# Attention values in quarters of the array, behind the query projections

## What is computed

```
x = x + _L0_conv_ref(_gn(x), ...)      # window attention and ffn
x = x + _L1_conv_ref(_gn(x), ...)      # patch network
# in the first, for windows of 8 x 8 pixels and 4 heads of 16 channels:
qkv = xw @ qkv_w + qkv_b
q, k, v = jnp.split(qkv, 3, axis=-1)
scores = jnp.einsum('bhqd,bhkd->bhqk', q, k)     # divided by the norms of q and k, and by tau
attn = jax.nn.softmax(scores + bias + mask)
out = jnp.einsum('bhqk,bhkd->bhqd', attn, v)
out = out.transpose(0, 2, 1, 3).reshape(B * NW, TOK, C) @ proj_w + proj_b
```

## Time and profile before

| | us |
|---|---|
| median of 3 runs | 784.1 |
| lowest, highest | 783.03, 784.84 |
| span of the profiled execution | 778.6 |
| TensorE busy | 665.7 (86%) |
| VectorE busy | 516.4 (66%) |
| ScalarE busy | 480.4 (62%) |
| GpSimd busy | 355.1 (46%) |

### The profile page before, as it was taken

The page is one execution under the profiler, slowest core; times in us unless marked ns, Lnnn a source line. Parts: engine busy times, 40 slices in busy tenths (PEclk is TensorE's granted clock), DMA queues, the critical chain, the costliest instruction groups (busy, mean ns, idle before and its releaser), DMA issues. The chain is left out here.

```text
span 778.6 us, 21192 instructions
## 1 busy us (share of the span) xinstructions
PE 665.7 (86%) x8584; PEld 371.4 (48%) x8584; DVE 516.4 (66%) x997; ACT 480.4 (62%) x963; POOL 355.1 (46%) x441
## 2 busy tenths in 40 slices
PE   4785789999999999999998579999999988749880
PEld 2562455565565555655555232233333367735350
DVE  4796487877777787877778322577777786372181
ACT  3565266777777777777775548877777656624000
POOL 4696446778777777788776520022221123100000
PEclk9787599999999999999999959999999999969955
DMA  9550000000000000000000020122112220120278
GB/s 216 137 128 11 1 3 2 3 2 3 2 3 3 3 3 3 3 2 3 3 2 3 2 56 1 28 55 56 33 50 55 55 55 2 31 72 2 63 194 269
DMA packets 15719, 31.44 MB, mean 40 GB/s; under 512 B 7488, under 2 KB 9284, under 8 KB 15620
## 3 DMA queue, kind: packets, MB, share of 16 engines
q1 hardware_dynamic: 12592, 29.16, 14.1%
q10 hardware_dynamic: 2760, 0.66, 0.5%
q0 software_dynamic: 272, 0.27, 0.2%
HBM read 20.71 MB, written 9.37 MB: 39 GB/s over the span
## 5 line engine op out<-in xcount | busy, mean ns | idle before, releaser
L794 POOL TENSOR_TENSOR sc<-sc,mx 128x512 f32<-128x512 f32 x128 | 133.7, 1044 | 102.4 <-DVE mx L725 102.4
L722 DVE TENSOR_TENSOR sc<-s_ps,bias_tab 128x512 f32<-128x512 f32 x128 | 87.7, 685 | 52.6 <-PE s_ps L528 52.6
L1424 POOL TENSOR_TENSOR square<-xs 128x1024 f32<-128x1024 f32 x16 | 34.1, 2133 | 165.5 <-DVE xs L1166 165.5
L539 PE MATMUL t_ps<-consts,sc 128*128 128x128 f32 x512 | 84.4, 288 | 16.2 <-ACT pt L656 12.5
L656 ACT ACTIVATE pt<-t_ps 128x512 f32<-128x512 f32 x128 | 75.7, 592 | 31.2 <-PE t_ps L539 30.1
L539 PEld LDWEIGHTS t_ps<-consts,sc 128*128 128x128 f32 x512 | 54.3, 142 | 84.8 <-issue 48.1
L725 DVE TENSOR_REDUCE mx<-sc 128x8 f32<-128x512 f32 x128 | 87.8, 686 | 4.4
L1081 ACT ACTIVATE hs<-h_ps,fb1s 128x512 f32<-128x512 f32 x128 | 78.2, 689 | 19.1 <-PE h_ps L990 19.0
L528 PE MATMUL s_ps<-kx,qu 32*64 32x128 f32 x2048 | 72.3, 278 | 3.5 <-DVE kx L749 2.9
L990 PE MATMUL h_ps<-xs,fw 64*128 64x512 f32 x256 | 68.7, 650 | 1.0 <-ACT hs L1081 1.0
L528 PEld LDWEIGHTS s_ps<-kx,qu 32*64 32x64 f32 x2048 | 56.7, 134 | 15.2 <-issue 13.4
(11 more groups left out here) (207 smaller groups left out, 1295.2 us busy)
## 6 DMA issues: line engine op xcount, KB each, us to landing
raw<-in_x_dram SPq DMA_DIRECT2D x32, 256.0 KB, 5.1
xr<-in_x_dram SPq DMA_DIRECT2D x32, 256.0 KB, 3.9
out_dram<-x SPq DMA_DIRECT2D x32, 256.0 KB, 3.9
rec_scratch<-r SPq DMA_DIRECT2D x4, 224.0 KB, 2.5
w<-in_L_conv_W_dram SPq DMA_DIRECT2D x1, 784.0 KB
w<-in_L_conv_W_dram SPq DMA_DIRECT2D x1, 672.0 KB
xs<-rec_scratch SPq DMA_DIRECT2D x16, 28.0 KB
xs<-rec_scratch ACTq DMA_DIRECT2D x16, 28.0 KB
```

The source lines that it names most:

```text
L539: last = pe.transpose(t_ps[:, m], sc[n % KEPT][:, m].rearrange("c h k -> c (h k)"), ident)
L722: dve.tensor_tensor(sc[n % KEPT][:, :, :, :], s_ps[j][:, :, :, :], bias_tab[:, j, hp], ALU.add)\
L794: pool.tensor_tensor(v, v, mx[n % KEPT][:, :].unsqueeze(2).broadcast_to([128, 8, TOK]), ALU.subtract)\
```

## The change

The value weights wv are no longer a 128 x 128 tile with zero blocks but 128 x 64, the weights once on each half of the rows; the memset of wv and its semaphore go. `values` takes one window of one image at a time (64 rows, 64 tokens) against 64 columns of weights. Where there were eight products over the whole array, there are 32, in turn on the four quarters. Bank a_ps[0] now holds the values of the lower image and a_ps[1] those of the upper, for both j; before, bank j held both images. `spread_values` copies by image accordingly, in the same number of operations of the same size. In `tensor_step` `values` moves from behind `turn(n - 2, 1)` to ahead of it, directly behind `project_queries`. In `scalar_step` the second `copy_queries` moves from the start of the next step to behind the first one, ahead of an exponent.

```
-        wv = sb(attention, "wv", [128, 128])
+        wv = sb(attention, "wv", [128, C])
...
-                          (wv[lo:hi, lo:hi], qkv_w[:, 2 * C:3 * C]), (pw[lo:hi, :], proj_w)]
+                          (wv[lo:hi, :], qkv_w[:, 2 * C:3 * C]), (pw[lo:hi, :], proj_w)]
...
-                    pool.memset(wv[:, :], 0.0).then_inc(zeroed, 1)
-                    pool.wait_ge(zeroed, 1)
...
                     for j in range(2):
                         for n in range(4):
-                            cols = slice(128 * n, 128 * (n + 1))
-                            last = pe.matmul(a_ps[j][:, cols], xu[:, 2 * p + j, cols], wv[:, :], start=True, stop=True)
+                            for w, (to_lo, to_hi) in enumerate(HALVES):
+                                at = slice(TOK * (2 * n + w), TOK * (2 * n + w + 1))
+                                for a, (lo, hi) in enumerate(HALVES):
+                                    last = pe.matmul(a_ps[a][to_lo:to_hi, C * (4 * j + n):C * (4 * j + n + 1)],
+                                                     xu[lo:hi, 2 * p + j, at], wv[lo:hi, :], start=True, stop=True)
...
-            def spread_values(act, p, j):
+            def spread_values(act, p, a):
...
-                    v = a_ps[j][:, :].rearrange("c (n g h d) -> c n g h d", n=4, g=4, h=2)
-                    to = vd[p % 2][:, WIN * j:WIN * (j + 1)].rearrange("c (n w) a p d -> c n w (a p) d", w=2)
+                    v = a_ps[a][:, :].rearrange("c (n g h d) -> c n g h d", n=8, g=2, h=2)
+                    to = vd[p % 2][:, :, a].rearrange("c (n w) p d -> c n w p d", w=2)
...
                 project_queries(pe, n - 1)
+                values(pe, n - 1)
                 turn(pe, n - 2, 1)
-                values(pe, n - 1)
                 score(pe, n - 2, 2)
...
-                copy_queries(act, n - 2, 1)
                 spread_values(act, n - 2, 0)
...
                 copy_queries(act, n - 1, 0)
+                copy_queries(act, n - 1, 1)
                 exponent(act, n - 2, 1)
```

More of the change, by code:

```diff
@@ L244, in build @@
             chain = sem(stage, "chain")
-            zeroed = sem(stage, "zeroed")
             hid_ps_ready = sem(stage, "hid_ps_ready")
```

## The result

The changed kernel takes 777.38 us (median of 4 runs, 777.09 to 777.86) against 783.62 for the kernel before (4 runs, 783.03 to 784.84): a ratio of 0.9927, 95% interval 0.9911 to 0.9943.

What follows compares the result with a forecast made beforehand. TensorE looked like the bound at 22.04 us a step, with a loop through VectorE and GpSimd at 21.91 close behind. Gains of 1.56 + 0.83 + 0.3 = 2.7 us took 784.1 to 781.4 us; range 779.5 to 785.0.

Steps and rivals of the forecast that it cites:

- The bound and the loop: Attention step: norms to spreading 4.27, to GpSimd's first subtraction 8.48, nine operations 9.04, signal 0.12; 21.91 us against 22.04.
- The values' cost: TensorE, line 489: 64 records on four quarters take 0.95 us, bounds 0.92 and 1.88, plus 0.09 for a shape change.
- The formula for transposition 4: ScalarE's queue lets transposition 4 start at 209.25 us plus the values' time; hidden by 0.38 us at 0.95.
- The sum in the stage: Attention stage: 1.56 us from twelve steps, 0.83 from two interrupted steps, 0.3 from the second pair; 2.7 us gained.
- The signal: From the end of GpSimd's squares to TensorE's norms, taken as 0.12 us; an ordinary step gains 0.13 us.
- The second pair: Attention stage, where ScalarE sets the pace and waits 1.35 us for the values: gain 0.3 us, bounds 0 and 1.35.
- The base: Whole kernel: median of the runs 784.1 us, 5.5 above the profiled span of 778.6, taken as the starting time.
- The first (loads not hidden): Transposition 4 waits behind ScalarE and steps lengthen: 786 to 790.0 us, from values of 1.46 us on; chance 14%.
- The second (interruptions in the loop): Nothing arrives: seven interruptions of 0.28 us in TensorE's part of the loop take 2.0 us; 783.4 us; chance 17%.
- The two interruptions of 0.28 us: Two steps where TensorE lost 0.28 us in another product; the loss falls into new idle time, gaining 0.42 + 0.41 us.
- The third (all of TensorE's gain): All 13 us of TensorE's gain arrives: 771 us, or 773 without the first pairs; needs a gap in GpSimd's row; chance 5%.
- a fall of the clock for 0.7 us: TensorE's new idle time ahead of the norms: no case of its own, since each step already has 0.78 us at 1.00.

Runs made afterwards that it cites:

- shortened: Second square of the projected output moved from GpSimd to VectorE: on the changed kernel 772.91 us, again 773.94; on the kernel before 782.26 us.
- the order alone: Kernel before with only the new order of values and query copies, values still eight products on the whole array: 787.87 us, 1.0069 of before.
- the first comparison: Changed kernel against the kernel before, four runs each: 777.38 us against 783.62, ratio 0.9927.
- the quarters alone: Changed kernel with the old order: values in quarters but behind transposition 1, second query copy behind the exponent: 777.04 us, 0.9947 of before.
- the longer loop: One more GpSimd operation of 1.04 us ahead of the last square, result unused: 795.04 us on the kernel before, 805.14 on the changed kernel.
- the repeated profile of before: Kernel before, unchanged, timed and profiled again: span 784.5 us, median 782.85 us of 12 runs, ratio 0.9994 against itself.
- The same square on ScalarE: Changed kernel with the second square of the projected output moved from GpSimd to ScalarE: 775.72 us, 0.9902 of before.

## Why the prediction was right and wrong

**The bound and the loop.** Right. Forecast 21.91 us from four pieces, measured 21.87: 4.26 (205.33 to 209.59), 8.48 (209.59 to 218.07), 9.03 (196.20 to 205.23), 0.10. The loop stood in the profile before the change as 0.25 us between squares and norms. Lengthened by one operation it gives 22.87 in both kernels, shortened it gives 0.49 to the changed kernel and nothing to the old one.

**The values' cost.** Right: 1.04 us against 0.95 + 0.09. The quarters load and stream side by side: line 489 before had a slot of 0.12 us for each record of 128 columns, so 64 records of 64 columns one behind the other would take 3.8 us by an estimate from it, and they took 1.04; their 64 loads, 0.13 us each, start within 1.2 us. The prediction also weighed a rule of some 25 ns between products (the Trainium skill, TensorE: Matmul & The Clock Gate, section "Wait — 56ns, not 53.3ns?"), by which, as an estimate, 64 records would have taken 1.6 us. The trace disagrees: 16 ns each.

**ScalarE.** The formula for transposition 4 was right in place and a little high: 0.25 us a step for the order alone, where it gives 0.33 to 0.42. With the short values it stayed hidden.

**The sum in the stage.** A little small. The signal took 0.10, not 0.12, so an ordinary step gains 0.16, not 0.13, and each of the two with an interruption 0.44. From the second pair's norms to the last this makes 2.9 us (307.84 to 304.95) where 2.4 was forecast. The second pair was set at 0.3 in bounds of 0 and 1.35; the profiles give 0.3 to 1.3 (22.22 and 21.37 us before, 20.93, 20.94 and 21.11 after); these steps lie where the clock still changes (granted 0.66 from 60 to 100 us in the first profile), but what part of the difference is the clock's is not shown. So 3.2 to 4.2 us, where 2.7 was forecast.

**The base, the step that failed.** "The median of the runs is 784.1, 5.5 above it" took the distance from span to median as if it belonged to the program, and three runs as its time. What lies around the span is 1.8 us. The other 3.7 us were the difference between the profiled execution and the three timed ones. A distance of 5.5 us was a sign of this, but one profile and three runs could not settle it. The prediction gave the unchanged kernel no scatter of its own, although the profile showed a first stage that runs at two clocks by turns (granted 0.63 to 0.86 in the ten-us stretches from 20 to 60 us): from one execution to another 4.8 us move there. Comparisons of the same two kernels gave 6.2, 1.5 and 3.2 us. Taken together, all 79 runs of before on record have a median of 782.5 and 24 of the changed kernel one of 778.9, 3.6 us apart, on several chips. So the change is worth about 3 to 4 us, and the rest of the first 6.2 us goes with the scatter. The size in the stage is shown for the profiled executions; the timed ones of the first comparison have no trace, and what part of them was lost where stays open.

The forecast of 781.4 us missed the 777.38 by 4.0. By these medians 1.6 of it are the base (784.1 for 782.5), 0.9 the size of the gain (2.7 for 3.6), and 1.5 the first four runs of the changed kernel, which lie that far below its median over all. So even without that last part the result would have lain under the range: a base too high and a gain too small added up.

**The rivals.** The first (loads not hidden) needed values over 1.46 us and fell, but its mechanism is real: it is what the order alone ran into. The second (interruptions in the loop) did not come: from the fourth norms on no step differs by more than 0.01 us. The two interruptions of 0.28 us of the kernel before were forecast to fall into the idle time. That they cost nothing is right, but for another reason: they did not occur. In those steps too, in all three profiles of the changed kernel, the idle time is its full 0.62 or 0.63 us. Why they are absent is not shown. That the idle time would have taken them is shown by the quarters alone, where 0.19 us of loss did. The third (all of TensorE's gain) fell.

## What to carry to other kernels

When the busiest engine is relieved, the gain ends at the shortest distance between some other engine's last input and its user, less what the signal takes (0.25 and 0.10 us here, so 0.15); find it by following the inputs backwards once round the loop, and add up the loop's pieces. The profile may call the new wait "issue"; a distance from producer to user that is equal in every step names the true source. And before a time is built on a profiled span, compare the median with it: if they differ by more than what lies around the span (1.8 us here), the profiled execution is not like the timed ones, and the range has to hold that scatter.

## What the runs showed of the hardware

**The clock fell behind longer idle time.** In the changed kernel with the longer loop (one execution) TensorE idles 1.63 us ahead of the norms. In six of the twelve later steps the work behind it ran at the lower clock for a while, and these steps took 24.4 to 24.5 us instead of 22.87. Stretches of the two kernels with the extra operation, the changed one first (the number behind the busy times is the granted clock):

```profile
233.00:239.00 6.00, 4.37 (x36) 2.02 (x28) 2.66 (x4) 4.10 (x11) 5.53 (x6) 0.72 0.01 1
```

```profile
233.00:239.00 6.00, 5.23 (x71) 3.35 (x72) 3.31 (x5) 4.50 (x12) 6.00 (x7) 1.00 0.01 4
```

With 0.77 us of idle time in the same place (the old kernel) or 0.63 (the changed one) no step did this, and six with 1.63 us did not either. So a link with the longer idle time is likely, but what tells the six steps from the others is not shown. The prediction had dismissed a fall of the clock for 0.7 us, rightly. Most of the 10.1 us by which the relieved kernel is slower than the one with more work stand in this stage: from the first norms to the last it takes 348.32 us against 339.93, 8.4 more.

**The granted clock can disagree with the durations.** In the repeated profile of before the record says

```profile
30.00:60.00 30.00, 27.92 (x350) 22.59 (x342) 25.13 (x92) 14.52 (x37) 22.34 (x86) 1.00 0.45 112
```

while the products of line 133 in this stretch take 421 ns each, what they take elsewhere at 0.50, and more than in the execution with 0.76 recorded there. The durations go with the time lost.

**VectorE's square and GpSimd slow each other.** The square, a product of two operands in SBUF, took 1.43 us on VectorE in fourteen of fifteen pairs; the last, with GpSimd idle for its second half, took 1.05. GpSimd's subtraction beside it took 1.49 us instead of 1.04. Not every operation of VectorE on SBUF does this: its maxima (line 725), which read one operand there, take 0.69 us beside GpSimd's 1.04. The same square on ScalarE took 0.63, with GpSimd's operations beside it at 1.04.
